# Graph convolution, last chunk cut three tiles and one, and layer norms measured by statistics instructions

## The reference

```
x = _layernorm(x + L0(x, adj, ...))          # gated cells on a graph attention
# L1:
sim  = tanh(adj * adj); filt = sim * (adj > 0)
new_adj = top 350 of each row of filt        # rows have far fewer, so all are kept
h2   = tanh(x @ W_proj + b_proj)
feat = relu(new_adj @ (h2 @ W_gcn) + b_gcn)
x = _layernorm(x + feat)                     # (x - mean) / sqrt(var + 1e-5)
```

## Time and profile before

| what | us |
|---|---|
| median of 3 runs (1340.47 to 1341.01) | 1340.59 |
| the profiled execution | 1340.1 |
| its span, first to last instruction or transfer | 1338.8 |
| PE busy in the span | 1319.6 (99%) |
| DVE busy | 1017.7 (76%) |
| ACT busy | 961.3 (72%) |
| mean granted TensorE clock, of full speed | 0.997 |

### The profile page before, as it was taken

One profiled execution on the slowest core, in us unless ns is written; L12 is line 12 of the kernel. 1 busy time (PEld: TensorE's weight loads), 2 busy tenths in 40 slices (PEclk: granted clock), 3 DMA queues, 4 the chain that ended last, 5 costly groups with the idle time before them and its releaser, 6 DMA issues.

```text
span 1338.8 us, 11264 instructions
## 1 busy us (share of the span) xinstructions
PE 1319.6 (99%) x3700; PEld 610.9 (46%) x3700; DVE 1017.7 (76%) x1331; ACT 961.3 (72%) x1087; POOL 93.3 (7%) x188
## 2 busy tenths in 40 slices
PE   8999999999999999999999999999999999999996
PEld 3444444464444444444444444444444454444455
DVE  2533333448798998999989999899968987788883
ACT  4655556238788988889888898898946666565662
POOL 0000001000000100100100100100103441000000
PEclk9999999999999999999999999999999999999998
DMA  9988887353123242332423424223123347888860
GB/s 370 361 288 283 299 290 279 73 206 135 70 95 141 95 160 92 110 141 95 142 94 106 162 79 151 101 94 104 53 94 108 128 146 251 306 292 308 299 219 18
DMA packets 46706, 228.92 MB, mean 171 GB/s; under 512 B 10610, under 2 KB 16434, under 8 KB 21042
## 3 DMA queue, kind: packets, MB, share of 16 engines
q1 hardware_dynamic: 44080, 225.55, 48.0%
q10 hardware_dynamic: 2562, 2.59, 0.6%
HBM read 223.83 MB, written 4.29 MB: 170 GB/s over the span
## 4 chain that ended last, share of the span: by engine, by line
PE 91%; DVE 4%; DMA 2%; POOL 1%; issue 1%; ACT 1%; SPq 0%; DVEq 0%; ACTq 0%; POOLq 0%
PE t_y_ps L1801 48%; PE ns_ps L422 15%; PE t_y_ps L1363 12%; PE t_y_ps L1779 4%; PE rows_ps L1363 3%; PE t_y_ps L1314 2%; DVE mask L1232 2%; PE t_es_ps L1770 2%; DMA pieces<-in_adj_c 2%; PE t_y_ps L1316 1%; PE pos_ps L436 1%; PE rows_ps L1316 1%; PE t_es_ps L1347 0%; DVE mask L1718 0%; PE t_y_ps L1340 0%
## 5 line engine op out<-in xcount | busy, mean ns | idle before, releaser
L1801 PE MATMUL t_y_ps<-mask,x_sb 128*128 128x512 f32 x1536 | 663.1, 592 | 0.3 <-DVE mask L1718 0.3
L1801 PEld LDWEIGHTS t_y_ps<-mask,x_sb 128*128 128x128 f32 x1536 | 290.1, 190 | 364.2 <-issue 343.0
L1718 DVE TENSOR_TENSOR mask<-mask 128x1536 f32<-128x1536 f32 x256 | 451.1, 1763 | 2.0 <-ACT mask L1602 2.0
L1602 ACT ACTIVATE mask<-mask,ones 128x1536 f32<-128x1536 f32 x256 | 400.3, 1564 | 0.0
L1595 ACT ACTIVATE mask<-mask,pieces 128x512 f32<-128x512 f32 x352 | 241.8, 713 | 31.3 <-PE t_y_ps L1801 28.2
L422 PE MATMUL ns_ps<-pieces,x_sb 128*128 128x512 f32 x504 | 226.3, 602 | 6.0 <-DMA pieces<-in_adj_c 5.6
L1704 DVE TENSOR_SCALAR mask<-mask,e_cols 128x512 f32<-128x512 f32 x416 | 189.2, 489 | 56.4 <-PE t_y_ps L1801 45.3
L1363 PE MATMUL t_y_ps<-mask 128*128 128x512 f32 (+1 forms) x448 | 181.2, 562 | 0.1
L422 PEld LDWEIGHTS ns_ps<-pieces,x_sb 128*128 128x128 f32 x504 | 93.8, 192 | 122.1 <-issue 115.6
L288 DVE TENSOR_SCALAR mask<-pieces 128x2048 fp8e4<-128x2048 f32 x64 | 76.9, 1224 | 92.8 <-DMA pieces<-in_adj_c 74.9
L1232 DVE SCALAR_TENSOR_TENSOR mask<-mask 128x2048 f32<-128x2048 f32 x64 | 142.4, 2285 | 0.9 <-DMA mask<-in_adj_c 0.9
(11 more groups left out here) (176 smaller groups left out, 635.3 us busy)
## 6 DMA issues: line engine op xcount, KB each, us to landing
mask<-in_adj_c SPq DMA_DIRECT2D x128, 1024.0 KB, 4.8
pieces<-in_adj_c SPq DMA_DIRECT2D x63, 1024.0 KB, 5.1
mask<-scratch_shifts SPq DMA_DIRECT2D x8, 1536.0 KB, 7.8
x_sb<-in_x_p SPq DMA_DIRECT2D x8, 256.0 KB, 8.9
mask<-in_x_t SPq DMA_DIRECT2D x1, 2048.0 KB, 17.0
pieces<-in_x_t SPq DMA_DIRECT2D x8, 256.0 KB, 2.9
pieces<-scratch_ns_t SPq DMA_DIRECT2D x8, 256.0 KB, 3.7
scratch_ns_t<-ns_sb ACTq DMA_DIRECT2D x7, 256.0 KB, 5.8
```

The lines of the kernel that those rows point to most:

```text
L1602: nc.scalar.activation(t, t, ACT.Exp, bias=ones[:, :], scale=-1.0).then_inc(exped, 1)
L1718: nc.vector.tensor_tensor(term(n), term(n), a, ALU.mult).then_inc(terms, 1)
L1801: mm = nc.tensor.matmul(y_ps[c % 2][h][:, :], x_sb[:, k, :], term(n)[:, h, :], start=k == 0, stop=k == NB - 1)
```

## The change

The last chunk is cut into three tiles and one (`END_PARTS`). The first part goes as before, with 384 columns. The last tile (`ROW_PARTS`) swaps the operands: the 128x128 tile of the unit is the weights and the 128 columns of `g_all` move, so that rows stand on the partitions and no transposes are needed. Its bias is added by a product first, a row of ones (one partition) by the row `b_gcn_row`, which a ninth weight DMA loads. DVE takes relu and the addition to x in one instruction from PSUM.

Both norms, all chunks: `center` and the squares on ACT go. DVE makes statistics (`bn_stats`) and mean and variance (`bn_aggr`) per tile (`measure`), and subtracts and multiplies in one instruction per tile (`normalize`). The buffer `squares` goes.

```diff
-END_PARTS = [(c, 0, CHUNK) for c in range(NCHUNK - 1)] + [(NCHUNK - 1, q, q + CHUNK // 2) for q in range(0, CHUNK, CHUNK // 2)]
+END_PARTS = [(c, 0, CHUNK) for c in range(NCHUNK - 1)] + [(NCHUNK - 1, 0, CHUNK - 1), (NCHUNK - 1, CHUNK - 1, CHUNK)]
+ROW_PARTS = (len(END_PARTS) - 1,)
...
+        sp.dma_start(b_gcn_row, dram["b_gcn"].unsqueeze(0)).then_inc(w_loaded, 16)
...
+        nc.vector.memset(one_row[:, :], 1.0).then_inc(bias_step, 1)
...
-            at, (sums, t, v, out) = POOL_STEPS * c, (a[:, rows(c)] for a in (square_sums, newton, var, root))
-            pool.wait_ge(squared, CHUNK * (c + 1))
-            nc.gpsimd.tensor_scalar(t, sums, 1.0 / H, EPS, ALU.mult, ALU.add).then_inc(rooted, 1)
-            nc.gpsimd.tensor_scalar(v, sums, -0.5 / H, -0.5 * EPS, ALU.mult, ALU.add).then_inc(rooted, 1)
+            at, spread, (t, v, out) = POOL_STEPS * c, moments[:, rows(c), 1], (a[:, rows(c)] for a in (newton, var, root))
+            pool.wait_ge(averaged, CHUNK * (c + 1))
+            nc.gpsimd.tensor_scalar(t, spread, 1.0, EPS, ALU.mult, ALU.add).then_inc(rooted, 1)
...
-        def square_x(c):
-            act.wait_ge(centered, 3 * (c + 1))
-            for t in range(c * CHUNK, (c + 1) * CHUNK):
-                if t:
-                    act.wait_ge(squared, t)
-                nc.scalar.activation(squares[:, t % CHUNK, :], x1[:, t, :], ACT.Square, accum_out=square_sums[:, t:t + 1]).then_inc(squared, 1)
...
-            if c >= 1:
-                square_x(c - 1)
...
-            if c < end and g == 4:
-                square_y(c - 1)
         relu(end - 1)
-        square_y(end - 1)
         for i in range(NCHUNK - 1, len(END_PARTS)):
-            relu(i)
-            square_y(i)
+            if i not in ROW_PARTS:
+                relu(i)
...
-        def center(i, y, mu, sem_centered):
-            count = mu.shape[1]
-            nc.vector.tensor_reduce(mu, y, AX_X, ALU.add).then_inc(sem_centered, 1)
-            dve.wait_ge(sem_centered, 3 * i + 1)
-            nc.vector.tensor_scalar(mu, mu, 1.0 / H, None, ALU.mult).then_inc(sem_centered, 1)
-            dve.wait_ge(sem_centered, 3 * i + 2)
-            nc.vector.tensor_tensor(y, y, mu.unsqueeze(2).broadcast_to([P, count, H]), ALU.subtract).then_inc(sem_centered, 1)
+        def measure(tiles, buf, out, sem_stats, sem_averaged):
+
+            for t in range(tiles.start, tiles.stop):
+                nc.vector.bn_stats(buf[:, t, :], x1[:, t, :]).then_inc(sem_stats, 1)
+            for t in range(tiles.start, tiles.stop):
+                dve.wait_ge(sem_stats, t + 1)
+                nc.vector.bn_aggr(out[:, t, :], buf[:, t, :]).then_inc(sem_averaged, 1)
+
+        def normalize(tiles, out, roots, sem_out):
+            for t in range(tiles.start, tiles.stop):
+                nc.vector.tensor_scalar(x1[:, t, :], x1[:, t, :], out[:, t, 0:1], roots[:, t:t + 1], ALU.subtract, ALU.mult).then_inc(sem_out, 1)
 
         def finish_x(c):
             dve.wait_ge(rooted, POOL_STEPS * (c + 1))
-            nc.vector.tensor_tensor(x1[:, rows(c), :], x1[:, rows(c), :], root[:, rows(c)].unsqueeze(2).broadcast_to([P, CHUNK, H]),
-                                    ALU.mult).then_inc(x_done, 1)
+            normalize(rows(c), moments, root, x_done)
...
+            if i in ROW_PARTS:
+                dve.wait_ge(products, NPIECE * (i + 1))
+                nc.vector.scalar_tensor_tensor(x1[:, tiles, :], f_ps[i % len(f_ps)][:, q * P:end * P].rearrange("p (r f) -> p r f", f=H), 0.0,
+                                               x1[:, tiles, :], ALU.max, ALU.add).then_inc(y2_done, 1)
+            else:
+                dve.wait_ge(turned2, i + 1)
+                nc.vector.tensor_tensor(x1[:, tiles, :], back_ps[i % 2][:, q * P:end * P].rearrange("p (r f) -> p r f", f=H), x1[:, tiles, :],
+                                        ALU.add).then_inc(y2_done, 1)
             dve.wait_ge(y2_done, i + 1)
-            center(i, x1[:, tiles, :], mean2[:, tiles], centered2)
+            measure(tiles, stats2, moments2, stats_made2, averaged2)
...
+                if i - len(f_ps) in ROW_PARTS:
+                    pe.wait_ge(y2_done, i - len(f_ps) + 1)
+                else:
+                    pe.wait_ge(relu_done, i - len(f_ps) + 1)
+            if g == 0 and i in ROW_PARTS and tiles.start == 0:
+                pe.wait_ge(bias_step, 9)
+                nc.tensor.matmul(f_ps[i % len(f_ps)][:, q * P:end * P], one_row[:, :],
+                                 b_gcn_row.unsqueeze(1).broadcast_to([1, end - q, H]), start=True, stop=False)
             for j in tiles:
                 k = g * PIECE + j
+                if i in ROW_PARTS:
+                    for r in range(q, end):
+                        mm = nc.tensor.matmul(f_ps[i % len(f_ps)][:, r * P:(r + 1) * P], piece(u)[:, j * CW + r * P:j * CW + (r + 1) * P],
+                                              g_all[:, k, :], start=False, stop=k == NB - 1 and r == end - 1)
...
+            graph(u, NCHUNK - 1, 0, CHUNK - 1)
             if u == end + 4:
                 turn_features(NCHUNK - 2)
         for u in range(end, NPIECES):
-            graph(u, NCHUNK, CHUNK // 2, CHUNK)
-            if u == end + 3:
+            graph(u, NCHUNK, CHUNK - 1, CHUNK)
+            if u == end + 1:
                 turn_features(NCHUNK - 1)
-        turn_features(NCHUNK)
```

More of the change, by code:

```diff
@@ L942 @@
 BUFFERS = ("edge_hid_n", "edge_r", "edge_z", "edge_n", "edge_cell", "both", "node_hid_n", "node_r",
[L943 removed]
+           "node_z", "node_n", "node_cell")
 BUFFER_SLOTS = (1, 2, 0)
[L945 removed]
+END_PARTS = [(c, 0, CHUNK) for c in range(NCHUNK - 1)] + [(NCHUNK - 1, 0, CHUNK - 1), (NCHUNK - 1, CHUNK - 1, CHUNK)]
+ROW_PARTS = (len(END_PARTS) - 1,)
 def tail_programs(nc, sem, dram, keep, banks, m):
@@ L959, in tail_programs @@
         {k: sem(f"h_{k}_{n}") for k in KINDS} for n in ("made", "read", "pre", "n", "cell"))
-    bias_step, cells, turned, y_done, centered, squared, rooted = (
-        sem("h_" + n) for n in ("bias_step", "cells", "turned", "y_done", "centered", "squared", "rooted"))
+    bias_step, cells, turned, y_done, stats_made, averaged, rooted = (
+        sem("h_" + n) for n in ("bias_step", "cells", "turned", "y_done", "stats_made", "averaged", "rooted"))
     x_done, x_turned, x_copied, projected, activated, multiplied, copied = (
@@ L964, in tail_programs @@
     squared_a, filtered, products = sem("h_squared_a"), sem("h_filtered"), sem("h_products")
-    relu_done, turned2, y2_done, centered2, squared2, rooted2, finished = (
-        sem("h_" + n) for n in ("relu_done", "turned2", "y2_done", "centered2", "squared2", "rooted2", "finished"))
+    relu_done, turned2, y2_done, stats_made2, averaged2, rooted2, finished = (
+        sem("h_" + n) for n in ("relu_done", "turned2", "y2_done", "stats_made2", "averaged2", "rooted2", "finished"))
     stored = keep["out_stored"]
@@ L978, in tail_programs @@
     hid_n, r, z, n, cell = ({k: buf[f"{k}_{name}"] for k in KINDS} for name in ("hid_n", "r", "z", "n", "cell"))
-    both, squares = buf["both"], buf["squares"].rearrange("p (r f) -> p r f", f=H)
+    both = buf["both"]
     feat_t = [hid_n["edge"], r["edge"]]
@@ L982, in tail_programs @@
     g_all = flat[:, G_AT:G_AT + N].rearrange("p (t f) -> p t f", f=H)
-    mean, mean2, square_sums, square_sums2, var, var2, root, root2, newton, newton2 = (
-        m.sb("h_" + k, [P, NB]) for k in ("mean", "mean2", "square_sums", "square_sums2", "var", "var2", "root", "root2", "newton", "newton2"))
+    var, var2, root, root2, newton, newton2 = (m.sb("h_" + k, [P, NB]) for k in ("var", "var2", "root", "root2", "newton", "newton2"))
+    stats, stats2 = (m.sb("h_" + k, [P, NB, 6]) for k in ("stats", "stats2"))
+    moments, moments2 = (m.sb("h_" + k, [P, NB, 2]) for k in ("moments", "moments2"))
     bias_cols = m.sb("h_bias", [P, len(KINDS), 4])
@@ L1064, in sync_tail @@
         for i in range(len(END_PARTS)):
-            sp.wait_ge(finished, i + 1)
+            sp.wait_ge(finished, part_rows(i).stop)
             sp.dma_start(out_rows[:, part_rows(i), :], x1[:, part_rows(i), :]).then_inc(stored, 16)
@@ L1119, in relu @@
             nc.scalar.activation(feat_t[i % 2][:, q * P:end * P], f_ps[i % len(f_ps)][:, q * P:end * P], ACT.Relu, bias=b_gcn).then_inc(relu_done, 1)
[L1121 to L1125, removed]
         act.wait_ge(bias_step, 8)
-        act.wait_ge(w_loaded, 16 * 8)
+        act.wait_ge(w_loaded, 16 * 9)
         for c in range(NCHUNK):
@@ L1259, in finish_y @@
             else:
-                nc.vector.tensor_scalar(var2[:, tiles], square_sums2[:, tiles], 1.0 / H, EPS, ALU.mult, ALU.add).then_inc(var_made, 1)
+                nc.vector.tensor_scalar(var2[:, tiles], spread, 1.0, EPS, ALU.mult, ALU.add).then_inc(var_made, 1)
                 dve.wait_ge(end_root, 2 * (i - ROOT_ON_ACT) + 1)
@@ L1263, in finish_y @@
                 dve.wait_ge(end_root, 2 * (i - ROOT_ON_ACT) + 2)
```

(7 more changed lines are left out.)

22 lines of the change are left out of this document (10 added, 12 removed).

## The result

The changed kernel takes 1332.32 us (median of 4 runs, 1330.96 to 1333.12), against 1340.80 of the kernel before (four runs, the three of the table above among them). The ratio is 0.9935, with a 95% interval from 0.9919 to 0.9950. Forecast were 1332.2 us and 8.4 us less. Two later sets of timings, on two chips, gave 0.9935 (0.9921 to 0.9948) and 0.9928 (0.9915 to 0.9942).

What follows compares the result with a forecast made beforehand. PE bounds the kernel (91% of the chain, 99% busy), except for its wait in the last chunk and the tail. 5.6 us there plus 2.7 in the tail, rounded to 8.4, gave 1332.2 us, range 1330.6 to 1336.0.

Steps and rivals of the forecast that it cites:

- PE's wait and the clock: PE's last chunk: without the wait at the transposes, 4.0 us of idle time and 1.9 of clock are gained.
- The length of the last chunk: PE, first to last product of the last chunk: 28.8 us against 34.39, 5.6 us less.
- C: Last sweep: weight loads bound it at 0.190 us a record, 5.2 us more, 1337.4 us; chance 0.05.
- E: Last sweep: loads not hidden at all, each record pays load and product, 12.2 us more, 1344.4 us; chance 0.02.
- The tail: Behind the last product to DVE's end: 1.82 us against 4.54, 2.7 us less.
- DVE's last chunk: DVE's norm in the last chunk: statistics part 1.45 us, normalizations 0.72, sum -0.06; bounds -0.7 and +2.0.
- The gate stage: Gate stage, where PE waited once, 1.1 us, for DVE's cells: counted 0, bounds -1.1 and +1.5.
- rival D: The gate stage's 1.1 us goes and the last transfer shrinks, 1330.8 us; chance 0.12.
- B: DVE's new instructions are dearer, PE's closed wait opens in part: 1333.4 us, or 1335.4; chance 0.17.
- F: Last chunk: PE waits as long as before, root's table load behind the last product, 1340.6 us; chance 0.02.
- A: Whole kernel as forecast, 1332.2 us, own range 1331.3 to 1333.4; chance 0.60.

Runs made afterwards that it cites:

- norms_only: The changed kernel with the last chunk in two halves as before, transposed, relu on ACT, so only the norms are by statistics; 1338.86 us, ratio 0.9980.
- gate_norm: The kernel before with only the first norm, in the gate stage, by statistics instructions; 1340.26 us, ratio 0.9993 (0.9984 to 1.0002).
- idle_back: The changed kernel with PE's transposes of the last chunk's wait behind the fourth unit, not the fifth; 1334.08 us, beside 1331.80 of the changed kernel.
- stats_twice: The changed kernel with every statistics instruction of the graph stage's norms issued twice; 1332.71 us, beside 1331.80 of the changed kernel.
- cut_transposed: The changed kernel with the last tile done as the others: transposes, relu on ACT, no row form, no bias product; 1332.02 us.
- cut_only: The kernel before with the last chunk cut three tiles and one, row form and bias product for the last, both norms as before; 1334.04 us, ratio 0.9948.

## Why the prediction was right

**PE's wait and the clock: right.** They were to give 5.9, and moving the transposes alone shortened the last chunk by 5.7, from 34.39 to 28.7 us. Bringing 2.3 us of the wait back cost 2.3 in the median and 2.5 in the last chunk. The clock's part rests on the kernels with 3.9 to 4.0 us of idle time (before, norms_only, gate_norm), the profiles of which all show the fall, and those without it, none of which shows it in the last chunk. Of the 1.9 that the prediction gave to the clock, 1.6 were in the products. The 0.3 in the transposes were charged to it wrongly for the most part: behind a wait at a clock of 1.00 the four took 0.66 us (idle_back, stats_twice), against 0.72 in the kernel before and 0.44 without a wait.

**The length of the last chunk: right, 0.5 short.** Predicted were 28.8, measured 29.34. The bias product took 0.41 where I had 0.22. The 64 records of the last sweep took 1.98 + 5.38 = 7.36 where I had 6.98. They came one every 0.112 us, on both sides of the transposes, where I had 0.109, which is 0.18 in all. The other 0.20 belong to the bias product too: the first of the records behind it comes that much late, and in cut_transposed, which has no bias product, none does. So the bias product put 0.61 us on PE's path where the prediction had 0.22. The last product ended at 1326.29 and not near 1325.5: 0.5 is this, and 0.3 is that the chunk began at 1296.95 and not at 1296.67. The loads are nearly hidden, and rivals C (0.190) and E (0.30) fall. By the rule of the Trainium skill (TensorE: Matmul & The Clock Gate, section The mechanism), that loads overlap only between different row groups, E would have held. The same section also lets a load go ahead into a background weight buffer, so the Trainium skill as a whole doesn't decide it. The trace disagrees with the rule: each of the 48 records has its own load in 0.112.

**The tail: right.** 1.82 predicted, 1.87 measured. A statistics instruction of 128 elements takes 0.28 and an aggregation 0.15 in the mean (busy us, mean ns of one in the view by form), and 0.29 and 0.18 alone in the tail:

```profile
L1213 DVE TENSOR_SCALAR x_sb<-x_sb,h_moments,h_root 128x128 f32<-128x128 f32 x64 | 17.9, 342 | 4.8 <-POOL h_root L1050 4.5
...
L1206 DVE BATCH_NORM_STATS2 h_stats<-x_sb 128x6 f32<-128x128 f32 x64 | 14.1, 281 | 0.6
...
L1209 DVE BATCH_NORM_AGGREGATE h_moments<-h_stats 128x2 f32<-128x6 f32 x64 | 5.9, 153 | 0.0
```

**DVE's last chunk: right in sum, wrong in its parts.** I had the statistics part at 1.45 and it took 1.07, since the four overlap to 0.20 each. I had the normalizations at 0.72 and they took 1.03, with 0.342 for one, by as much as 0.35 in the tail in place of 0.25. The sum of -0.06 came out as -0.13. The warning of the Trainium skill (VectorE: DVE Perf Modes, section on the TRN2 errata) against small tiles, charged in full, would have added 0.6. This trace doesn't agree with charging it in full: the two parts together took 2.10, not 2.84.

**The gate stage: the term that was mis-sized.** I counted 0 with bounds of -1.1 and +1.5, held that "the stall came with a square in DVE's list, which stays", and gave it to rival D. It is -1.3, beyond the bound, in all ten profiles with the new first norm (125.97 to 125.99) and in none of the three with the old (127.27 to 127.30). DVE is not slower in it, as the sum of its new instructions is about that of the old. What differs is the chain ACT, POOL, DVE before the stalled cells: the squares on ACT have gone, and in a window of the changed kernel DVE still has 35.30 busy of 40 us. Two links of that chain in the kernel before are these, squares of one chunk and the first step of its root:

```profile
1027.64 0.41 ACT pieces L1092 x2
...
1029.44 0.27 POOL h_newton L1033
```

That this chain was the cause is read from the chain of waits of before and wasn't tried by itself: gate_norm shows that the first norm is the cause, and not which of its instructions.

**Rivals B and F.** B's condition didn't come: statistics at 0.20 in a row where it asked for 0.5. It named the right place, as the doubled statistics show. F had the wait stay, which it did only where the widths and the order stayed.

That the median met the forecast to 0.1 us has luck in it. By the stretches the change is worth 9.05 us, not 8.4: the gate stage gave 1.3 more than I counted and the last chunk 0.5 less. Rival D's mechanism came true, at the time of A. The rest is scatter of the start. The three sets of timings gave 8.5, 9.3 and 9.4 us against 8.4.

## What to carry to other kernels

When PE is 99% busy, look for the one place where it is not, and ask what order put it there: here the work list reached an instruction 4 us before its input, and one position in the list was worth 5.7 of the 9.05 us of the whole change. Fill a wait with work that has to be done anyhow before making anything faster. Replace a hop between engines at the very end by an instruction on the engine that goes on, but price the bias or copy that this form needs, with what it does to its neighbours, for here the row form came out even.

## What the runs showed of the hardware

- With 3.9 to 4.0 us without work PE's granted clock fell, to 0.50 of full speed in a whole window of 3 us (the lower level, 1.2 GHz). In the kernel before it fell behind the wait and the last chunk took 34.39 us, in norms_only within it and the last chunk took 35.07. With 2.27 us without work it stayed at 1.00 in the one execution profiled (idle_back).
- Behind a wait the first four transposes took 0.66 us at a granted clock of 1.00, where they took 0.44 without a wait (idle_back, stats_twice, the changed kernel).
- A statistics instruction of 128 f32 elements from SBUF takes 0.29 us alone and one every 0.20 in a row; an aggregation of six numbers 0.18 and 0.07.
- Subtract-and-multiply with two per-partition scalars took 0.342 us for 128 elements, 0.26 in a row.
- Products of 128 columns with full 128x128 f32 weights came one every 0.112 us, each with its own weights. A product of two such records with one row of weights, put between full ones, took 0.41, and the next 16 records 0.20 more than without it.
- The root on ACT took 0.29 us with a bias column and 0.20 without. The load of its table took 1.28 us: hidden in the changed kernel, between the last square and the root of part 7 in cut_only.
